# q, latent, k and v as three f16 products of high and low halves, loops at a block's head, and new orders for all engines, in a fused attention and quantized-FFN kernel

## What is computed

```python
q = x @ Wq
latent_kv = (x @ Wk + x @ Wv) @ W_down_kv
k_rec, v_rec = latent_kv @ W_up_k, latent_kv @ W_up_v
scores = einsum('bhqd,bhkd->bhqk', heads(q), heads(k_rec)) * scale      # clipped to +-10000
scores = scores * exp(-0.0001 * abs(i - j))                              # clipped again
out = softmax(scores) @ heads(v_rec) @ Wo
z = quantize(x1n @ H) @ ternary(weight).T
```

## Time and profile before

| | |
|---|---|
| median of 3 runs | 1436.37 us (1433.69, 1436.37, 1437.82) |
| profiled execution, first to last instruction | 1433.2 us |
| opening, until the first scores | 33.7 us |
| iterations 0, 1, 2, 3 | 38.0, 41.1, 41.3, 43.6 us |
| iterations 4 to 29 | mostly 41.8, at most 42.3 us |
| iterations 30 and 31 | 43.6 and about 43 us |
| after the last iteration | about 58 us |
| TensorE busy | 94% |
| VectorE, ScalarE, GpSimd busy | 82%, 77%, 58% |

### The profile page before, as it was taken

One profiled execution on the slowest core, in us unless ns is written; L12 is line 12 of the kernel. 1 busy time (PEld: TensorE's weight loads), 2 busy tenths in 40 slices (PEclk: granted clock), 3 DMA queues, 4 the chain that ended last, 5 costly groups with the idle time before them and its releaser, 6 DMA issues.

```text
span 1433.2 us, 35971 instructions
## 1 busy us (share of the span) xinstructions
PE 1349.5 (94%) x12330; PEld 600.5 (42%) x12330; DVE 1179.9 (82%) x2739; ACT 1098.2 (77%) x1125; POOL 834.7 (58%) x1238
## 2 busy tenths in 40 slices
PE   5889999999999999999999999999999999999863
PEld 3334444444444444444444444444444444443332
DVE  7567888888888888888888888888888888888655
ACT  1878787888888788878878887887888787787831
POOL 4223655666565666556557655656765655675446
PEclk9999999999999999999999999999999999999986
DMA  6455456556555645656564565655556555555420
GB/s 194 154 167 170 154 172 202 155 164 206 164 182 173 197 156 166 206 157 190 173 190 157 173 201 157 193 175 187 156 177 194 163 185 184 176 156 175 128 77 31
DMA packets 174557, 241.45 MB, mean 168 GB/s; under 512 B 28336, under 2 KB 145200, under 8 KB 174512
## 3 DMA queue, kind: packets, MB, share of 16 engines
q1 hardware_dynamic: 140176, 206.78, 46.5%
q10 hardware_dynamic: 34336, 34.08, 7.7%
HBM read 154.80 MB, written 69.21 MB: 156 GB/s over the span
## 4 chain that ended last, share of the span: by engine, by line
PE 76%; DVE 8%; issue 5%; ACT 4%; DMA 3%; SPq 2%; POOL 2%; DVEq 0%; ACTq 0%; POOLq 0%
PE heads_ps L720 27%; PE scores_ps L707 16%; PE misc_ps L603 8%; PE misc_ps L635 7%; PE misc_ps L660 4%; PE misc_ps L614 3%; PE misc_ps L587 3%; ACT probs L909 2%; DVE x_hl L1204 2%; PE misc_ps L595 2%; PE misc_ps L678 2%; DVE diagonal L1253 2%; DVE weighted L1161 2%; PE misc_ps L625 2%; PE misc_ps L669 1%
## 5 line engine op out<-in xcount | busy, mean ns | idle before, releaser
L909 ACT ACTIVATE probs<-scores_ps 128x1024 f32<-128x1024 f32 x768 | 759.8, 1026 | 248.0 <-PE scores_ps L707 247.9
L720 PE MATMUL heads_ps<-probs,v_sb 128*32 128x512 f32 x4096 | 525.4, 603 | 3.6 <-DVE heads L1150 1.9
L1253 DVE TENSOR_TENSOR diagonal<-scores_ps,comp 128x1024 f32<-128x1024 f32 x256 | 312.2, 1219 | 70.1 <-PE scores_ps L707 70.1
L707 PE MATMUL scores_ps<-q_rep,k_rep 64*128 64x128 f16 (+2 forms) x5120 | 324.6, 251 | 16.0 <-DVE diagonal L1253 9.2
L707 PEld LDWEIGHTS scores_ps<-q_rep,k_rep 64*128 64x128 f16 x5120 | 165.6, 94 | 348.7 <-DVE diagonal L1253 149.5
L916 ACT ACTIVATE probs<-diagonal 128x2048 f32<-128x2048 f32 x128 | 246.0, 1922 | 0.0
L996 POOL TENSOR_TENSOR ln_neg_mean<-zero,ln_moments 128x4 f32<-128x4 f32 (+1 forms) x131 | 34.6, 264 | 356.5 <-DVE ln_moments L1115 356.3
L1161 DVE SCALAR_TENSOR_TENSOR weighted<-misc_ps,edges 128x384 f32<-128x384 f32 x256 | 129.4, 547 | 64.3 <-PE misc_ps L603 33.8
L720 PEld LDWEIGHTS heads_ps<-probs,v_sb 128*32 128x32 f32 x4096 | 91.5, 108 | 171.7 <-issue 169.8
L1038 POOL TENSOR_TENSOR q_hl<-weighted,q_hl 128x768 f16<-128x768 f32 x64 | 105.5, 1648 | 77.5 <-DVE q_hl L1168 77.5
L1043 POOL TENSOR_TENSOR heads_c<-heads_c,den_spread 128x1024 f32<-128x1024 f32 (+1 forms) x33 | 75.7, 2296 | 111.0 <-DMA den_spread<-den_scratch 111.0
(11 more groups left out here) (132 smaller groups left out, 1511.5 us busy)
## 6 DMA issues: line engine op xcount, KB each, us to landing
q_rep<-q_scratch SPq DMA_DIRECT2D x128, 384.0 KB, 4.3
k_rep<-k_scratch SPq DMA_DIRECT2D x256, 192.0 KB, 3.9
q_scratch<-q_hl SPq DMA_DIRECT2D x64, 384.0 KB, 2.6
k_scratch<-k_hl SPq DMA_DIRECT2D x64, 384.0 KB, 3.1
x_in<-in_L_attn_x_dram ACTq DMA_DIRECT2D x32, 512.0 KB, 4.9
heads_c<-heads SPq DMA_DIRECT2D x256, 64.0 KB, 2.5
x_res<-in_L_attn_x_dram ACTq DMA_DIRECT2D x32, 512.0 KB, 6.8
den_spread<-den_scratch SPq DMA_DIRECT2D x256, 64.0 KB, 2.3
```

What stands on the lines that cost most here:

```text
L707: ins = mm(scores_ps[:, place + par, at:at + n * P], k_rep[rows, pair, kv_, k_cols], q_rep[rows, pair, qv_, q_cols], start=True, stop=True)
L720: ins = mm(heads_ps[W32 * g:W32 * (g + 1), :], v_sb[:, b.slot, kt, at:at + W32], probs[:, quad % 2, g, kt, :], start=(kt == 0), stop=(kt = ...
L909: nc.scalar.activation(flat[:, :, at:at + S], scores_ps[:, place:place + 2, :], ACT.Exp, scale=EXP_SCALE).then_inc(off_probs, 1)
L1253: v.tensor_tensor(diagonal[:, quad % 2, 2 * two:2 * two + 2, :], scores_ps[:, place:place + 2, :], comp[:].rearrange("p t n -> p (t n)").u ...
```

## The change

`xT` and the latent are no longer kept in f32 but as two f16 halves: ScalarE copies the PSUM bank to f16 (`x_high_take`, `lat_high_take`, both new), VectorE subtracts that from the bank and writes the low half, where it copied the bank before. The weights become high and low f16 halves too, scaled by 1024, once, in the opening. Each f32 product becomes three f16 products, high with high, high with low and low with high, summed in PSUM. v is scaled back as it is taken from PSUM, q and k in the factor they had. The test that picks the fast path also bounds the weights (`WEIGHT_BOUND`). The loop's first instruction is put at slot 0 of an instruction block on each engine. All five orders are new; the last y-projection wait of `compact` moves into it, and the f32 path stays for the general path (`b.buffers == 1`).

```diff
+PRODUCTS = ((0, 0), (0, 1), (1, 0))
...
             def lat_stage(b, part, piece):
...
+                    for c in range(DC):
+                        for n, (wh, xh) in enumerate(PRODUCTS):
+                            for half in range(2):
+                                ins = mm(misc_ps[LAT * half:LAT * (half + 1), bank, 0:S // 2], w_lat_hl[:, wh, c, :],
+                                         xT_hl[:, xh, c, half * S // 2:(half + 1) * S // 2], start=(c == 0 and n == 0),
+                                         stop=(c == DC - 1 and n == len(PRODUCTS) - 1))
...
             def q_stage(b, part, piece):
...
+                    for n, (wh, xh) in enumerate(PRODUCTS):
+                        ins = mm(misc_ps[:, BANK["q", part], :], wq_hl[:, wh, piece, part * P:(part + 1) * P], xT_hl[:, xh, piece, :],
+                                 start=(piece == 0 and n == 0), stop=(piece == DC - 1 and n == len(PRODUCTS) - 1))
...
+            def x_high_take(b, part):
+                act.wait_ge(in_psum["xT"], part_count("xT", b, part))
+                nc.scalar.activation(xT_hl[:, 0, part, :], misc_ps[:, BANK["xT", part], :], ACT.Copy).then_inc(x_high, 1)
+
+            def lat_high_take(b, part):
+                act.wait_ge(in_psum["lat"], part_count("lat", b, 0))
+                nc.scalar.activation(latT_hl[:, 0, :], misc_ps[:, BANK["lat", part], 0:S // 2], ACT.Copy).then_inc(lat_high, 1)
...
+                dve.wait_ge(x_high, part_count("xT", b, part))
+                v.tensor_tensor(xT_hl[:, 1, part, :], bank, xT_hl[:, 0, part, :], ALU.subtract).then_inc(taken["xT"], 1)
...
+                        ins = v.tensor_scalar(dst, src, 1.0 / W_GAIN ** 2, None, ALU.mult)
...
-            with eng.Fori(0, (B - 6) // 2) as loop:
+            with nc.Fori(0, (B - 6) // 2, engines=[eng.engine], head_slot={eng.engine: 0}) as loop:
...
 TENSOR_STEPS = {
-    1: [("z", 0, 0), ("z", 1, 0), ("pv_end", 3, 0)], 3: [("xT", 0, 0), ("pv_end", 3, 1)], 5: [("xT", 1, 0), ("pv_end", 3, 2)],
+    1: [("xT", 0, 0, "pre"), ("xT", 1, 0, "pre"), ("z", 0, 0, "c")], 3: [("pv", 3, 0, "a")], 5: [("pv", 3, 1, "a")],
...
 VECTOR_STEPS = {
...
-    18: [("heads", 0), ("act_scales",)], 20: [("v", 1), ("x_stats",), ("x_moments",), ("q_split", 1)], 25: [("heads", 1)],
...
+    26: [("x_stats", "load")], 28: [("x_moments", "load"), ("y", 0, "a"), ("y", 1, "a")], 29: [("y_stats", "a")], 31: [("y_moments", "a")],
```

More of the change, by code:

```diff
@@ L61 @@
 DISTANCE_OF = {"load": 2, "pre": 1, "own": 0, "a": -1, "b": -2, "c": -3}
[L62 to L70, removed]
@@ L71 @@
-DISTANCE = {stage: DISTANCE_OF[group] for stage, group in GROUP.items()}
+PRE = ("xT", "lat", "q", "k", "v")
 STEPS = 32
 TENSOR_STEPS = {
[6 rows of a table removed]
[7 rows of a table added]
 }
 SCALAR_STEPS = {
-    4: [("load_res", 0)], 12: [("x1T", 0)], 14: [("x1T", 1)], 15: [("load_x", 0)], 21: [("round_x", 0)],
-    22: [("round_x", 1), ("round_x", 2), ("round_x", 3)], 30: [("qintT", 0)],
+    6: [("xT", 0, "pre"), ("xT", 1, "pre")], 10: [("load_x", 0, "load"), ("lat", 0, "pre")], 11: [("x1T", 0, "b")], 14: [("x1T", 1, "b")],
+    20: [("load_res", 0, "a"), ("round_x", 0, "b")], 23: [("round_x", 1, "b")], 25: [("round_x", 2, "b"), ("round_x", 3, "b")],
+    30: [("qintT", 0, "b")],
@@ new lines @@
+    19: [("v", 1, "pre"), ("act_scales", "b")], 21: [("heads", 1, "own")], 25: [("q", 1, "pre"), ("quantize", "b")],
+    26: [("x_stats", "load")], 28: [("x_moments", "load"), ("y", 0, "a"), ("y", 1, "a")], 29: [("y_stats", "a")], 31: [("y_moments", "a")],
+}
+POOL_STEPS = [
+    ("x1_apply", "b"), ("q", 0, "pre"), ("rstd4", "c"), ("k", 0, "pre"), ("k", 1, "pre"), ("add_out", "c"), ("heads_normalize", "a"),
+    ("q", 1, "pre"), ("x_apply", "load"), ("rstd2", "a"),
+]
+SYNC_STEPS = [
+    ("own", "spread", 1), ("a", "gather_den"), ("a", "compact", 1), ("a", "pack_den"), ("pre", "store_q", 0), ("a", "return_den"),
+    ("pre", "store_k", 0), ("a", "spread_den"), ("pre", "spread", 0), ("pre", "store_k", 1), ("own", "compact", 0), ("pre", "store_q", 1),
+    ("c", "store_out"),
+]
@@ L471, in compact @@
                 sp.wait_ge(heads_done, opened + count(HQ, b, 2 * (half + 1)))
+                if half == 0 and b.buffers == 2 and not (isinstance(b.number, int) and b.number == 0):
+                    sp.wait_ge(in_psum["y"], part_count("y", b.other(-1), 1))
                 for g in range(4):
@@ L527, in iteration @@
                     if present[group]:
-                        if step == "compact" and part[0] == 0 and present["a"]:
-                            sp.wait_ge(in_psum["y"], part_count("y", b.other(-1), 1))
                         steps[step](b.other(DISTANCE_OF[group]), *part)
@@ L736, in iteration @@
                         scores(b, h, not post_a)
-                    for stage, part, piece in TENSOR_STEPS.get(h, []):
-                        if present[GROUP[stage]]:
-                            stages[stage](b.other(DISTANCE[stage]), part, piece)
+                    for stage, part, piece, group in TENSOR_STEPS.get(h, []):
+                        if present[group]:
+                            stages[stage](b.other(DISTANCE_OF[group]), part, piece)
             def enter_loop(loop, b):
@@ L745, in enter_loop @@
                     await_taken(*held)
-                for stage, part, _ in ORDER_ALL:
-                    before = b.other(DISTANCE[stage] - 1)
+                for stage, part, _, group in ORDER_ALL:
+                    before = b.other(DISTANCE_OF[group] - 1)
                     holder[BANK[stage, part]] = (stage, part, before)
@@ L782, in weight_norms @@
                                  start=(ci == 0), stop=(ci == DC - 1))
+                pe.wait_ge(w_squared, 1)
+                mm(scores_ps[:, 3, D:2 * D], ones, sq_up[:, 0, :], start=True, stop=False)
+                for ci in range(DC):
+                    mm(scores_ps[:, 3, D:D + LAT], ones, sq_lat[:, ci, :], start=False, stop=False)
+                ins = mm(scores_ps[:, 3, D:2 * D], ones, sq_up[:, 1, :], start=False, stop=True)
                 ins.then_inc(setup_pe, 1)
@@ L856, in general_path @@
                             ins.then_inc(g_pv, 1)
[L857 removed]
+                    for stage, part, piece, _ in GENERAL_ORDER["after"]:
                         stages[stage](b, part, piece)
@@ L921, in iteration @@
                 for h in range(STEPS):
-                    for stage, part in SCALAR_STEPS.get(h, []):
-                        if present[GROUP[stage]]:
-                            takes[stage](b.other(DISTANCE[stage]), part)
+                    for stage, part, group in SCALAR_STEPS.get(h, []):
+                        if present[group]:
+                            takes[stage](b.other(DISTANCE_OF[group]), part)
                     if own and h % 4:
@@ L1261, in iteration @@
                         weigh_diagonal(b, h // 4, not post_a)
-                    for step, *part in VECTOR_STEPS.get(h, []):
-                        if present[GROUP[step]]:
-                            steps[step](b.other(DISTANCE[step]), *part)
+                    for step, *part, group in VECTOR_STEPS.get(h, []):
+                        if present[group]:
+                            steps[step](b.other(DISTANCE_OF[group]), *part)
             def ternary_weights():
```

180 lines of the change are left out of this document (119 added, 61 removed), and 24 rows, old and new, of tables (TENSOR_CLOSING, TENSOR_STEPS, VECTOR_STEPS).

## The result

| | before | after |
|---|---|---|
| median | 1437.53 us (6 runs) | 1448.88 us (6 runs, 1446.26 to 1452.81) |
| ratio | | 1.008, 95% interval [1.006, 1.010] |
| profiled execution: span | 1433.2 us | 1444.4 us |
| first scores | 33.7 us | 34.9 us |
| iterations 0 to 2 together | 120.4 us | 119.6 us |

0.8% slower. The forecast was 1427, faster than before, and its range ended at 1443. One run of the variant b_old took 3386.54 us; it is in no median and no ratio here, and no profile of it was taken.

What follows compares the result with a forecast made beforehand. Bound by TensorE's own time, 41.32 of 41.80 us a batch. 41.8 - 2.5 + 2.2 = 41.5, over 28 batches -8.5; with the rest -9: 1424 profiled, median 1427, range 1398 to 1443.

Steps and rivals of the forecast that it cites:

- TensorE's work: f16 products for q, latent, k and v, k's waits and seams: 2.5 us a batch less, 41.8 to 39.3.
- rival D: Each f16 weight load stands bare ahead of its matmul: 2.3 us a batch more, 1490 us; chance 0.01.
- What is given back: Waits from the new orders at pair 1, xn and step 13: 2.2 us a batch, bounds 0 to 3.0.
- Pair 1: With scores and only one pv it is shorter than its two exponentials; pair 2's second scores wait 0.6 us.
- xn: x_moments now follows step 28's decay product, so pair 0's transposes wait for xn: 0.9 us, between 0.65 and 1.2.
- Step 13 with x1T: Step 13's scores wait 0.75 us for ScalarE to pass exponential 11; x1T's lateness of about 0.4 lies inside that.
- rival C: GpSimd's heads_normalize, now behind k's second split and add_out, is late for y: 1447 at 1 us late; slower side 0.24.
- Rival A: Waits cover each other, late pair 0 shortening step 13's: 0.7 given back, 1385, halfway 1405; chance 0.18.
- Rival B: All is given back: waits of 2.5 to 2.6 us, batches 41.7 to 41.9, 1432 to 1440; chance 0.16.
- Iterations 0 to 2: Same products and fewer of the waits: -0.3 us each, -1 together.
- Opening: VectorE has four more operations ahead of its first xT, q gives 0.5 back: +0.5 us, between -0.5 and +1.5.
- The head: Loop's first instruction placed at an instruction block: 0 gained, with 3 us for the batches that are a little longer.

Runs made afterwards that it cites:

- b_old: The changed kernel's f16 products with all engines in the orders of the kernel before; 1419.7 us (three runs), ratio 0.988 to the kernel before.
- a_split: Changed kernel with the addition of x1, the last part of GpSimd's add_out, moved behind heads_normalize; 1414.3 us, ratio 0.984 to the kernel before.
- a_xmom: Changed kernel with VectorE's x_moments back behind x_stats at step 26 instead of behind step 28's decay product; 1433.5 us, ratio 0.998.
- a_pair1: Changed kernel with the second transposes of xn in pair 1, as in the kernel before, instead of pair 0; 1450.5 us, ratio 1.009.
- b_comb: Changed kernel with a_split's and a_xmom's moves, x1_moments ahead of VectorE's two xT subtractions, quad 3's second and third pv a pair earlier; 1427.8 us, ratio 0.994.
- c_pv0: Changed kernel with a_split's and a_xmom's moves, plus quad 0's first three pv a pair earlier on TensorE; 1415.8 us, ratio 0.986.

## Why the prediction failed

Point by point, in the batch of 663.36:

- **TensorE's work: right, a little too careful.** Distances beyond the usual ones add up to 3.7 us: pair 0 0.55, pair 2 0.67, x1T 0.44, step 13 0.46, pair 9 0.17, and 1.41 at pair 11 and the scores behind it. So TensorE alone takes 42.4 - 3.7 = 38.7, where the text had 39.3; before had 0.85 of waits in its batch by the same reckoning, not the 0.43 at k that the text took out. No f16 weight load stood bare: rival D did not take place, and the rule of the Trainium skill behind it (TensorE: Matmul & The Clock Gate, Part 3, "What overlaps and what doesn't") does not hold for these loads, by q's 1.40 for six products (6 x 0.216 + 0.10, and nothing for a load).
- **What is given back.** Pair 1: 0.6 forecast, 0.67. xn: 0.9 forecast, 0.55, the lower bound of 0.65 being nearer; xn went at 2.18, not 2.72. Step 13 with x1T: 0.75 forecast, 0.44 + 0.46 = 0.90. Sum 2.12, the text had 2.2.
- **The step that failed is the list of places, "Three places, per batch".** A fourth was never priced: what the new place of `add_out` on GpSimd does to VectorE. The text followed `add_out` only to y (rival C) and took VectorE's operations at their lengths of before whatever runs beside them ("VectorE subtracts where it copied, at the same length, 36.1"); it was busy 37.4. With 39.3 + 2.2 right to 0.6 and 1.4 left out, 41.5 became 42.4. Taken away again (a_split), the whole is 1414, at 13 us from the forecast. The trace of before held the warning, though not in the batch that the prediction read. In its closing the same operation, on two numbers per partition, stands beside the same addition:

```profile
1413.80 2.34 POOL L1056 TENSOR_TENSOR out_sb<-out_sb,x 128x1024 f32<-128x1024 f32 x1
...
1413.82 2.35 DVE L1217 TENSOR_SCALAR xscale<-absmax 128x2 f32<-128x2 f32 x1
```

  And 27 of the 64 casts of q took more than 0.6 us there, with a median of 1.02, where one alone takes 0.56.
- **Rival C** had the sign and even the mover (`add_out` behind k's splits) but the wrong victim: `heads_normalize` ended at 693.95 (691.59 + 2.36) and y started at 695.72. The 0.24 that the prediction gave to slower came true by a mechanism that it did not have: luck, as far as the reason goes.
- **Rival A** (the waits cover each other): not so for a_split and a_xmom, whose gains add up. It holds for moves inside TensorE's list (a_pair1, b_comb, c_pv0): there a wait taken away comes back at another place, most often for ScalarE's exponentials.
- **Rival B** (all is given back): the three places gave back 2.12 us, not the 2.5 that it needs; with the fourth, 3.7 were given back, more than it had.
- **The rest.** Iterations 0 to 2: -1 forecast, -0.8. Opening: +0.5 forecast, +1.2. The head: "0, with 3 us" was the price beside the old loop; in the new one it is worth 78.

## What to carry to other kernels

When a step moves on GpSimd, list what VectorE does in its new place: an operation of VectorE from SBUF to SBUF, however small, may last as long as the GpSimd operation beside it. Here that was so for scaling by constants, for casts and for the form with two inputs, not for the statistics of the layernorms. An engine's busy time that rises without new work is the sign to look for, and the operation's own median against its length of before finds the culprit in one view. Before work of TensorE is moved ahead of some scores, look whether ScalarE stands idle for them: work put there can delay ScalarE by its whole length (1.00 us for the `pv` in c_pv0). A loop that grew may need its head placed: compare the packets of the instruction queue with and without.

## What the runs showed of the hardware

- An operation of VectorE of 128x4 elements, 0.17 us alone, stood 2.0 to 2.3 us beside GpSimd's addition from SBUF and ended with it. Counted over the whole trace of after: 30 xscale began beside a GpSimd operation, median 2.23; 3 did not, 0.17. Of the operations with a source in PSUM, those that began beside one of GpSimd kept their length (absmax 61 times, 0.68; v 121 times, 0.41; the decay product 98 times, 1.22). So did the statistics of x_in, from SBUF, beside the split of q (118 times, 0.41). In b_old 25 casts of q, 0.56 us alone, took more than 0.6, with a median of 1.02 and a longest of 1.54.
- It goes the other way too. In after, 29 splits of q on GpSimd began while VectorE's rounding (0.69 us, from SBUF) was running, and took 2.03 to 2.04 us; the other 35 took 1.64 to 1.66.
- The Trainium skill (SBUF — State Buffer, "SBUF: two separate sides") calls the port pair that the two engines share an "exclusive lock", held for the whole instruction by whichever starts first: a GpSimd operation, or a VectorE operation in a two-port mode or (against a GpSimd operation that reads SBUF, as the addition does) with two inputs in SBUF. By the Trainium skill (VectorE: DVE Perf Modes, "What auto-detection actually checks") a single source and the destination in SBUF with even or equal outer widths give such a mode; it names no stride among the conditions of that mode. The traces agree in all three: the plain form (2.03 us, mean of 31), the strided one (2.02) and the one with two inputs (2.01) were all held up.
- Two waits of 2.5 and 2.7 us a turn for the loop's own instructions, and 9 packets of them, in a loop whose head was not placed, though the same kernel with its head at slot 0 fetches nothing in its turns. The loop of before did without: 27 packets in all, and 1436.8 us with the head placed against 1437.3.

What stays open: that ScalarE sets the pace from exponential 5 to about step 19 is read from idle times and waits, and no run takes work off ScalarE alone. Nor was a move tried that puts the `pv` behind the scores that ScalarE waits for. What shortened iterations 3 and 30 is not known either.
